# A four-layer recommender head in split fp32 on one core: weight splitting moved from GpSimd to VectorE and ScalarE, with the start of the kernel reordered

## What is computed

```python
# r_bottom_output: (2048, 27, 128)
interaction = jnp.einsum('bnd,bmd->bnm', bottom_output, bottom_output)
interaction_flat = interaction[:, _TRIL_R, _TRIL_C]          # 351 pairs
x = jnp.concatenate([bottom_output[:, 0, :], interaction_flat, zero_pad], axis=1)   # 480 wide
x = relu(x @ W0.T + b0)    # 1024
x = relu(x @ W1.T + b1)    # 1024
x = relu(x @ W2.T + b2)    # 512
x = relu(x @ W3.T + b3)    # 256
return x @ W4.T + b4       # 1
```

## Time and profile before

| | us |
|---|---|
| median of 3 runs (498.1 to 499.6) | 499.39 |
| the profiled execution's own time | 496.88 |
| its span in the trace | 495.1 |
| TensorE busy | 469.9 (95%) |
| VectorE busy | 284.7 (57%) |
| ScalarE busy | 241.4 (49%) |
| GpSimd busy | 45.6 (9%) |

### The profile page before, as it was taken

One profiled execution on the slowest core, in us unless ns is written; L12 is line 12 of the kernel. 1 busy time (PEld: TensorE's weight loads), 2 busy tenths in 40 slices (PEclk: granted clock), 3 DMA queues, 4 the chain that ended last, 5 costly groups with the idle time before them and its releaser, 6 DMA issues.

```text
span 495.1 us, 6689 instructions
## 1 busy us (share of the span) xinstructions
PE 469.9 (95%) x2480; PEld 399.0 (81%) x2480; DVE 284.7 (57%) x487; ACT 241.4 (49%) x579; POOL 45.6 (9%) x27
## 2 busy tenths in 40 slices
PE   6999678799999999999999999999999999999996
PEld 5999567687888888788888888788888888888874
DVE  3695899767734777766615777757624633110123
ACT  3987277566663357565653357565553321110121
POOL 0436440122320000000000000000000000000000
PEclk9999889999999999999999999999999999999999
DMA  7994055477339141455245141455224100434200
GB/s 270 392 402 167 0 166 212 141 279 289 130 138 344 38 142 39 177 204 197 85 168 212 55 124 56 156 187 212 86 85 132 41 0 1 170 100 156 85 0 2
DMA packets 17456, 72.28 MB, mean 146 GB/s; under 512 B 2448, under 2 KB 2448, under 8 KB 13328
## 3 DMA queue, kind: packets, MB, share of 16 engines
q1 hardware_dynamic: 17424, 71.86, 40.6%
HBM read 63.45 MB, written 8.40 MB: 145 GB/s over the span
## 4 chain that ended last, share of the span: by engine, by line
PE 83%; DVE 9%; issue 3%; ACT 3%; DMA 1%; SPq 1%; DVEq 0%; ACTq 0%
PE work L730 16%; PE work L732 16%; PE work L731 16%; PE gps L755 9%; PE acc L730 7%; PE acc L732 7%; PE acc L731 7%; PE acc L742 2%; PE gps L742 2%; DVE pairs L589 1%; DMA xraw<-x_t 1%; DVE xs L537 1%; ACT grams L413 1%; ACT grams L429 1%; DVE featH L544 1%
## 5 line engine op out<-in xcount | busy, mean ns | idle before, releaser
L413 ACT ACTIVATE grams<-gps 32x216 f32<-32x216 f32 x384 | 131.2, 342 | 94.8 <-PE gps L755 91.3
L730 PE MATMUL work<-h1h,w1s 128*128 128x512 f32 x256 | 101.2, 395 | 0.0
L732 PE MATMUL work<-h1l,w1s 128*128 128x512 f32 x256 | 100.4, 392 | 0.0
L731 PE MATMUL work<-h1h,w1s 128*128 128x512 f32 x256 | 100.1, 391 | 0.0
L445 ACT ACTIVATE act_out<-work,bias 128x512 f32<-128x512 f32 (+1 forms) x64 | 42.3, 661 | 97.5 <-PE work L732 94.7
L755 PEld LDWEIGHTS gps<-xs 128*128 128x128 f32 x384 | 57.0, 191 | 21.1 <-issue 7.8
L755 PE MATMUL gps<-xs 128*128 128x224 f32 x384 | 59.2, 277 | 10.7 <-DVE featL L617 4.2
L626 DVE CAST h2h<-act_out 128x512 fp32r<-128x512 f32 x40 | 17.1, 427 | 79.0 <-ACT act_out L445 79.0
L555 DVE SCALAR_TENSOR_TENSOR grams<-grams 128x216 f32<-128x216 f32 x48 | 19.3, 402 | 72.2 <-ACT grams L413 72.2
L730 PE MATMUL work<-featH,w0l 126*128 126x512 f32 (+5 forms) x160 | 57.8, 362 | 0.6 <-ACT act_out L452 0.4
L732 PEld LDWEIGHTS work<-h1l,w1s 128*128 128x128 f32 x256 | 48.0, 188 | 10.6
(11 more groups left out here) (65 smaller groups left out, 559.8 us busy)
## 6 DMA issues: line engine op xcount, KB each, us to landing
xraw<-x_t SPq DMA_DIRECT2D x64, 432.0 KB, 4.9
w1s<-w_parts SPq DMA_DIRECT2D x24, 1024.0 KB, 4.8
w_parts<-w1s SPq DMA_DIRECT2D x8, 1024.0 KB, 5.7
stage<-w_t SPq DMA_DIRECT2D x8, 512.0 KB, 6.4
w0raw<-w_t SPq DMA_DIRECT2D x4, 512.0 KB, 7.2
w2raw<-w_t SPq DMA_DIRECT2D x4, 512.0 KB, 6.8
x0raw<-x_t SPq DMA_DIRECT2D x4, 256.0 KB, 4.3
w3raw<-w_t SPq DMA_DIRECT2D x1, 512.0 KB, 6.8
```

Of the source, the lines that this page charges most:

```text
L413: last = act.activation(grams2[rows, h // 2 % 2, at:at + HALF_GROUPS, :, :], src[:, :, :, q * EVEN:q * EVEN + INPUTS], ACT.Copy)
L730: pe.matmul(dst, wl, ah, start=start, stop=False)
L731: pe.matmul(dst, wh, ah, start=False, stop=False)
L732: return pe.matmul(dst, wh, al, start=False, stop=stop)
```

## The change

- **Weights.** GpSimd keeps only the identity matrix. The 17 low parts of weights (W0 4, W2 4, W3 1, W1 8) and the four memsets of `xs`'s pad columns are VectorE's, at places written out by hand. ScalarE's high parts are at new places too.
- **W0 by columns.** A piece of W0 is now all four input blocks of 256 columns (two output tiles), and `layer0_left` waits for piece m/2 only.
- **SP's order.** The first six slices go out one behind the other, the three small loads (biases, W4, b4) behind slice 5, W0's pieces behind slices 7, 9, 11 and 12, x0 behind slice 8, then the first two input slices of chunk 1, two of W1, two more slices, and then W2 and W3.
- **First banks.** Up to slice 11 the Gram matrices go round over three pairs of banks (`work` is the third). Transposes stand after slices 7, 11, 15. 13 transposes of the identity are issued on PE before the first Gram matrix.
- **Chunk 0's weave.** The halves of chunk 1 stand after steps 6, 11, 16, 21, 26 and then every 3, with a transpose 2 steps ahead of the next half; the last transpose stands inside the first tile of layer 0 of chunk 1 (`late_turn`), behind its dense block. `input_parts` runs two slices ahead there, not three. The plan of chunks 1 and 2 is as it was.
- **Layer 4** goes by input rows: for each input tile its high part and then its low part, each as its own group of four matmuls with its own columns, each with its own wait; the sum over eight columns is in `tensor_reduce`.

```diff
+        def plan(starts, gap, last):
+
+            half_at, turn_at, step = {}, {}, None
+            for h in range(HALVES):
+                step = starts[h] if h < len(starts) else step + 3
+                sub, behind = divmod(h - 1 - TURN_BEHIND, 2 * SLICES_SUB)
+                if behind == 0 and sub >= 0:
+                    turn_at[step] = sub
+                    step += gap
+                half_at[step] = h
+            turn_at[last] = SUBS - 1
...
+        plans = [plan([6, 11, 16, 21, 26], 2, STEPS)] + [plan([1], 3, STEPS - 6)] * (CHUNKS - 2) + [({}, {})]
...
-        W0_AFTER = [1, 3, 5, 7]
-        W23_AFTER = [11, 12, 13, 14, 15]
-        HI_BEHIND = 2
+        SMALL_AFTER = 5
+        W0_AFTER = [7, 9, 11, 12]
+        W0_HI_AFTER = [6, 9, 11, 13]
+        W0_LO_AT = [8, 10, 13, 14]
+        DENSE_AT = 9
+        W4_AT = 10
+        WARM = 13
         PAD_AHEAD = 2
-        TRANSPOSE_AT = SLICES_SUB + 2
+        TRANSPOSE_AT = SLICES_SUB + 3
...
-            return acc[:, 0:2, :] if p % 2 else gps[:, :, :]
+            banks = gps[:, :, :], acc[:, 0:2, :], work[:, :, :]
+            return banks[p % 3 if p < LEFT_AT else p % 2]
...
-            load_x(0, 0)
-            sp.dma_start(w4raw[:, :, :], w4).then_inc(small_in, 16)
-            sp.dma_start(bias[:, :], biases).then_inc(small_in, 16)
-            sp.dma_start(bias4[:, :], b4.to_broadcast([P, 1])).then_inc(small_in, 16)
-            for p in range(1, SLICES):
+            for p in range(SLICES):
                 load_x(0, p)
+                if p == SMALL_AFTER:
+                    sp.dma_start(bias[:, :], biases).then_inc(small_in, 16)
...
-            def w1_lo(m):
-                pool.wait_ge(w_hi, REST + m + 1)
-                pool.tensor_tensor(w1s[:, m % 2, 1, :], stage[:, m % 2, :], w1s[:, m % 2, 0, :].bitcast(f32),
-                                   ALU.subtract).then_inc(w_done, 1)
...
+            def w0_lo_part(n):
+                dve.wait_ge(w0_hi, n + 1)
+                dve.tensor_tensor(w0_piece(w0l, n), w0_piece(w0raw, n), w0_piece(w0h, n).bitcast(f32),
+                                  ALU.subtract).then_inc(w0_done, 1)
...
+            zero_pads(0)
+            input_parts(1, 0)
             first_pairs(SUBS - 1)
...
+                    if c == 0 and m + 2 < MT1:
+                        w1_lo_part(m + 2)
+                    if c == 0 and m % 2 == 0:
+                        w2_lo_part(m // 2)
+                    if c == 0 and m == MT1 - 1:
+                        w3_lo_part()
...
                 pe.wait_ge(w4_done, 1)
-                pe.wait_ge(split_done, nth(c, 3, MT3 - 1, more) + 1)
-                for s in range(SUBS):
-                    for k in range(MT3):
...
+                for k in range(MT3):
+                    n = nth(c, 3, k, more)
+                    for part, (h2, ready) in enumerate(((h2h, hi_done), (h2l, split_done))):
+                        pe.wait_ge(ready, n + 1)
+                        for s in range(SUBS):
+                            at = ((s * MT3 + k) * 2 + part) * 2
+                            last = pe.matmul(acc[:, 3, at:at + 2], h2[:, k, s * SUB:(s + 1) * SUB], w4s[:, k, :],
+                                             start=True, stop=True)
...
             pe.wait_ge(ident_done, 1)
+            for _ in range(WARM):
+                pe.transpose(acc[:, 3, 0:P], ident[:, :], ident[:, :])
```

More of the change, by code:

```diff
@@ L209, in rec_program, with before @@
         STEPS = L0_STEPS + L1_STEPS + MT2 * KT2
-        APART_STEPS, TURN_STEPS = 3, 6
         TURN_BEHIND = 10
[L212 to L224, removed]
+        def plan(starts, gap, last):
[8 more added lines that the diff above has]
+            turn_at[last] = SUBS - 1
+            assert sorted(turn_at.values()) == list(range(SUBS)) and max(half_at) < last <= STEPS
+            return half_at, turn_at
+        plans = [plan([6, 11, 16, 21, 26], 2, STEPS)] + [plan([1], 3, STEPS - 6)] * (CHUNKS - 2) + [({}, {})]
+        def before(c, step):
+            half_at, turn_at = plans[c]
             return (sum(x < step for x in half_at), sum(x < step for x in turn_at))
         LEFT, RIGHT = slice(0, CHUNK // 2), slice(CHUNK // 2, CHUNK)
-        W0_AFTER = [1, 3, 5, 7]
-        W23_AFTER = [11, 12, 13, 14, 15]
-        HI_BEHIND = 2
+        SMALL_AFTER = 5
[5 more added lines that the diff above has]
+        WARM = 13
         PAD_AHEAD = 2
-        TRANSPOSE_AT = SLICES_SUB + 2
+        TRANSPOSE_AT = SLICES_SUB + 3
         LEFT_AT = 2 * SLICES_SUB + 4
@@ L284, in interleave @@
             passed(MT2)
+            if STEPS in turn_at:
+                on_turn(turn_at[STEPS])
         @block.sync
@@ L332, in _ @@
+            for m in range(2):
+                load_w1(m)
+            for p in range(2, XSLOTS):
+                load_x(1, p)
+            for n in range(W2_LOADS):
+                sp.dma_start(w2_part(w2raw, n), w2[n, :, :]).then_inc(w2_in[n], 16)
+            sp.dma_start(w3raw[:, :], w3).then_inc(w3_in, 16)
             load_x0(1)
-            for p in range(XSLOTS):
-                load_x(1, p)
             def body(c):
                 more, later = c + 1 < CHUNKS, c + 2 < CHUNKS
[L338 to L343, removed]
+                for m in range(2 if c else 0):
+                    refill_w1(c, m)
+                if c == 0:
+                    x_before_keep = {0: (4, 5), 1: (6, 7), 2: (8, 9), 3: (10, 11), 4: (12, 13), 5: (14, 15)}
+                elif more:
@@ L347, in body @@
                     if c == 0:
+                        for p in x_before_keep.get(m, ()):
+                            load_x(c + 1, p)
                         keep_w1(m)
@@ L350, in body @@
                             load_w1(m + 2)
[L351 to L355, removed]
+                    else:
+                        if m + 2 < MT1:
+                            refill_w1(c, m + 2)
+                        for p in loads_at(m) if more else []:
+                            load_x(c + 1, p)
+                    if later and m == (3 if c == 0 else 0):
                         load_x0(c + 2)
@@ L693, in on_tile @@
                             answers(c - 1)
+                        if c == 0 and m == MT0 - 1:
+                            w1_lo_part(1)
                     else:
@@ L770, in transpose_pairs, with once, step @@
                 last.then_inc(pairs_t, 1)
+            def once(what):
+                left = [what]
+                def step():
+                    if left:
+                        left.pop()()
+                return step
             def layer0_products(m, samples, after_step=lambda: None):
@@ L820, in layer2 @@
                 pe.wait_ge(split_done, nth(c, 1, k) + 1)
+                if c == 0 and k % 2 == 0:
+                    pe.wait_ge(w2_done, k // 2 + 1)
                 for m in range(MT2):
```

185 lines of the change are left out of this document (102 added, 83 removed).

## The result

| | before | after | after, a second measurement |
|---|---|---|---|
| median, us (range; runs) | 499.39 (498.1 to 499.6; 4) | 485.1 (484.07 to 487.04; 4) | 483.96 (483.72 to 485.19; 5) |
| ratio to before, 95% interval | | 0.972, 0.969 to 0.976 | 0.970, 0.967 to 0.972 |
| the profiled execution's own time | 496.88 | 487.04 | 483.79 |
| its span | 495.1 | 485.3 | 482.0 |
| TensorE / VectorE / GpSimd busy | 469.9 / 284.7 / 45.6 | 472.1 / 282.9 / 0.7 | |

485.0 us was predicted. The kernel became 14.3 us faster, as forecast, and VectorE's busy time did not rise although it took over 17 subtractions (20.7 us at 1.22 each) and four memsets (1.3): without these after's VectorE would be busy for 260.9 us, so before's was held for an estimated 284.7 - 260.9 = 23.8 us. All 17 are VectorE's now; ScalarE still makes the high parts, at new places. The sum is less exact than the hit looks.

A forecast was written before the change was run, and what follows sets the result against it. TensorE was taken to wait in the first 95 us, largely for VectorE copies held by GpSimd's subtractions. Terms 5.5 + 9.1 - 1.5 + 1.3 = 14.4 off the median 499.4 gave 485.0 us, range 480.5 to 491.

The forecast's parts named there:

- Step 1: Front part: body of chunk 0 starts at 53.4 us against 58.98, 5.5 gained; bounds 9.8 and 0.7.
- Step 2: Layer 0 in chunk 0's body: 10.7 us instead of 21.58, with four halves (1.8) left for later; 9.1 gained.
- Step 3: Rest of chunk 0: waits of 2.8 and 0.4 go, new ones of 4.7 come; 1.5 lost.
- Step 4: Layer 4: twelve of 16 small matmuls lie in the wait of 2.06 us, four behind the last split; 1.3 gained.
- The mechanism: VectorE's copies stand still while GpSimd subtracts; this pattern stands before TensorE's waits of 3.39, 2.74 and 2.8 us.
- it doesn't free VectorE: Rival, chance 0.03: VectorE's stretches have another cause than GpSimd; only layer 4 and the first slices gain: 496 us.
- the chain to slice 11: Front part: queued ScalarE and VectorE work ends with slice 11's copy at 27.1 us; TensorE, done at 24.9, waits 2.3.
- I take 2.1: First Gram slice: 2.1 us, between 1.8 if the 13 transposes warm the array fully and 3.5 if not at all.
- cold waits: Rival, chance 0.22: transposes don't warm the array (1.4), waits of 2.3 and 1.6 each lower the clock (3.4): 489.8 us.
- the 4.7 that I listed: Rest of chunk 0: new TensorE waits for ScalarE, behind the first transpose, at later turns and at the end, 4.7 us.
- Loads and W0's pieces: Front part: column pieces of W0 and reordered loads hidden, all at nothing; up to 1 us at half the load rate.
- The table load: ScalarE's table load: 1.28 us by the row; with the skill's DRAIN behind it, the time would be 0.9 longer.

The follow-up runs named there:

- e5: The kernel after, unchanged, measured a second time beside other runs on the same chip: 483.96 us, ratio 0.970.
- e11: Kernel after plus 17 GpSimd subtractions of 128x1024 on a spare tile that nobody waits for: 503.49 us, ratio 1.009.
- e8: Kernel before with only the 17 low parts and the memsets moved from GpSimd to VectorE: 499.87 us, ratio 1.002.
- e3: Kernel after with chunk 0's weave undone, so it gets the plan of the other chunks: 493.79 us, ratio 0.989.
- e1: Kernel after without the 13 transposes ahead of the first Gram matrix: 486.82 us, ratio 0.975.
- e12: e9 with the paddings of the third and fourth slot ahead of W1's first low part and the second input's split: 482.57 us, ratio 0.968.
- e9: Kernel after with sub-chunk 1's padding and second input split written later, behind the seventh left feature tile: 484.52 us, ratio 0.971.
- e7: Kernel after with padded copies three slices ahead and W3's low part two tiles of layer 1 earlier on VectorE: 486.66 us, ratio 0.974.
- e4: Kernel before with the new layer 4 only: 498.14 us, ratio 0.996.
- e2: Kernel after with the 17 subtractions back on GpSimd, VectorE keeping the memsets: 496.5 us, ratio 0.994.

## Why the prediction held, step by step

| step | predicted | after's profile | e5's profile |
|---|---|---|---|
| 1: body of chunk 0 starts earlier | 5.5 | 0.9 (58.10) | 3.95 (55.03) |
| 2: layer 0 in that body, four halves left | 9.1 | 8.6 | 8.7 |
| 3: rest of chunk 0 | -1.5 | -1.1 | -0.9 |
| 4: layer 4, and all behind it | 1.3 | 1.35 | 1.4 |
| sum, in spans | 14.4 | 9.8 | 13.1 |
| in medians | 14.4 | 14.3 | 15.5 |

The columns are differences of stage ends: for step 3, 90.02 us before (80.56 to 170.58) against 92.87 and 92.75, less 1.8 for the four halves.

- **The mechanism** (GpSimd's subtractions hold VectorE's copies) was right, and e11 shows it by itself. The rival "it doesn't free VectorE" is out. But of the three waits that I put down to it, only the one of 3.39 goes when the engine alone is changed (e8). Where VectorE has the subtractions and the old weave is kept, waits of the other two kinds are there again: 2.74 for split inputs and 1.7 for `featL` in e8, 3.5 for `featL` in e3. They needed the new order as well.
- **Step 1, the chain to slice 11.** The queue that I wrote out is the one that ran: high features, low features, copy of slice 10, pairs of sub 1, W0's low part, copy of slice 11. VectorE in after:

```profile
24.78 0.56 DVE L623 TENSOR_TENSOR featL<-acc,featH 126x384 fp32r<-126x384 f32 x1 [4.26 <-ACT featH L438]
25.26 0.60 DVE L678 COPY xpad<-xraw 128x864 f32<-128x864 f32 x1
25.77 1.88 DVE L590 STREAM_TRANSPOSE turned<-grams 128x864 f32<-128x864 f32 x1
27.68 0.66 DVE L594 COPY pairs<-turned 128x144 f32<-128x144 f32 x5
28.26 1.22 DVE L653 TENSOR_TENSOR w0l<-w0raw,w0h 128x1024 fp32r<-128x1024 f32 x1
29.39 0.60 DVE L678 COPY xpad<-xraw 128x864 f32<-128x864 f32 x1
```

  The last copy ends at 29.99; in e5 TensorE goes on at 27.80, in my sum at 27.2. The wait was 2.1 for 2.3. The next, of 0.5 for low features, measured 0 in after and 0.7 in e5, and the one of 1.6 before the first right tile 1.9 in both.
- **Step 1, the term that was mis-sized.** "I take 2.1" for the first slice: it took 3.55 in after and 2.56 in e5, and the second was cold too in after (2.94 for 1.79): 2.6 us beyond my term. Behind the wait at slice 11 after has a lower clock as well: it takes 28.05 us from there to the body, e5 27.23 with a wait of 0.7 that after has not, so 1.5 more. That is 4.1 of the 4.6 us between 5.5 and 0.9. In e5 the part fell 1.6 short of the sum: 0.6 at slice 11, most of it from the first slice, and 1.0 behind it, of which 0.5 are the waits. The profiled executions of after, e1 and e12 had the lower clock behind a wait of 2.1, those of e5 and e9 did not. The windows from 31 to 33 us of after and of e5:

```profile
31.00:33.00 2.00, 2.00 (x12) 2.00 (x12) 2.00 (x4) 0.14 (x1) 0.00 (x0) 0.54 0.81 238
```

```profile
31.00:33.00 2.00, 1.30 (x12) 1.16 (x11) 1.23 (x4) 1.96 (x5) 0.00 (x0) 1.00 0.79 229
```

  The wait ahead was 2.10 us in both. So "cold waits", my first rival (4.8 us), is what after's profiled execution had, for 4.6 us less than the sum, and e5's had little of. Its parts were of other sizes: the cold slices cost 2.6 for 1.4, and the clock fell once, for 1.5, where the rival has it fall twice for 1.7 each; behind the wait of 1.9 it stayed at 1.00. It is a difference between executions of one kernel, not between two outcomes of the change.
- **Step 2** came nearly as summed: 11.16 and 11.08 us for 10.7. The one wait for a relu is 0.55, for 0.4.
- **Step 3** has the right size by two errors. The waits were smaller than the 4.7 that I listed, 2.6 in e5: 0.8 behind the first transpose for 1.4, 0.5 ahead of it for ScalarE's 0.9, none at two later ones for 0.6, 1.17 + 0.18 at the end for 1.3 + 0.5. "W3's low part" in that 1.3 was wrong, as e7 shows: it is hidden, and the wait is the way out of the transpose alone. The 1.3 isn't the sum of the three steps named for it either: 0.49, 1.23 and 0.56 are 2.3, which would have made the forecast 486.0. In return some 1.5 us are spent beyond the waits and the four halves: TensorE's busy time in the stage is 90.17 in e5 against 86.88 before, 1.5 more when the halves' 1.8 are taken off. Six half slices show 0.68 instead of 0.60 in the timeline, where before has two, which accounts for some 0.3. The rest stays open.
- **Step 4** was right, by e4 too.
- **Loads and W0's pieces** at nothing: no wait for a slice or a piece of W0 stands in after's list but 0.2 at the first padded copy. **The table load**: the Trainium skill ("ScalarE: Activation LUTs", section "What ACT_TABLE_LOAD costs") has a DRAIN of 1380 ns behind it. The trace does not agree: 1.28 us, and the next ACTIVATE 0.02 behind its end. The sum was right to keep the row.

```profile
8.54 1.28 ACT L430 ACT_TABLE_LOAD   x1 [8.54 <-PE gps L789]
9.84 1.40 ACT L430 ACTIVATE grams<-gps 32x216 f32<-32x216 f32 x4
```

- **From sum to median.** I took the 14.4 off the median of before, as if both kernels' profiled executions stood equally to their medians. Before's stood 2.5 below its median, after's 1.9 above, e5's 0.2 below. Span against span the sum was 1.3 too high (e5) or 4.6 (after); against the medians it is 0.1 too high or 1.1 too low. So the hit within 0.1 us is luck. Why before's other executions are slower than its profiled one is only partly on record. The granted clock goes with it: of the 63 executions of before beside the experiments, the 13 with a mean of 0.990 or more have a median span of 497.4, the 32 with 0.986 or less one of 498.6, and the profiled one had 0.991 and 495.1. That is about 1 us; the rest is open.

## What to carry to other kernels

Look at GpSimd and VectorE side by side in the timeline before counting an engine as free: here an instruction on GpSimd cost VectorE more time than doing the same work on VectorE (30.4 us in e2 and 22.9 in e11, against 20.7), even when nobody needed its result. A move to another engine and the order around it have to be tried together, since here they gave 0 and 3 us by themselves, and 14 together. And when a wait moves instead of going, read in the program which counter the waiting engine asks for, and up to what number: e9 became e12 by one loop.

## What the runs showed of the hardware

- GpSimd's subtraction of 128x1024 holds VectorE's copies and two-input instructions, on data that the two don't share: in e11 a VectorE subtraction takes 2.13 us for 0.43 beside one of 1.89, and the next copy, behind GpSimd's end, 0.28 again. The transpose kept its time (1.98 for 1.95). The Trainium skill says it in "SBUF — State Buffer", section "Who interferes with whom": a VectorE instruction with two SBUF inputs contends with a GpSimd instruction that reads SBUF, a copy in a two-port mode contends too, and whoever comes second is blocked for the whole instruction of the other, not slowed. The trace agrees, with an estimated 30.4 us of such blocking in e2 and 22.9 in e11; in which mode a copy ran no row shows.
- The same 13 transposes left the array cold for two slices, for one or for none in different executions, and the same wait of 2.1 us was followed by a granted clock of 0.54 in one execution and 1.00 in another. Some 3 us of difference between two profiled executions of one file come from these two.
- The granted clock doesn't show the cold slices: it reads 1.00 over the first slice of before, of after and of e1. In after a matmul of that slice takes 421 ns and a weight load 333 (medians), and 275 and 192 for the slice at 22.24, at a granted clock of 1.00 both times.
